# Post-norm transformer layer on eight cores: where the feed-forward weights' bf16 halves are cast from, and two waits of TensorE on VectorE

## The reference

```python
# x: (8, 2048, 1024) f32; one sequence per core
def reference(x, Wq, Wkv_down, Wk_up, Wv_up, Wo, W1, b1, W2, b2, scale):
    q = (x @ Wq.T).reshape(b, t, 8, 256)
    kv_latent = x @ Wkv_down.T                       # rank 64
    k, v = up-projections of kv_latent, 8 heads of 256
    attn = softmax(q k^T * 256 ** -0.5); out = attn v, concatenated @ Wo.T
    x = layernorm(x + out)
    # feed-forward, H = 4096, D = 1024
    lt = x[:, 1:17, :]; even, odd = lt[:, ::2], lt[:, 1::2]
    m1 = (even[:, :4, :, None] * odd[:, :4, None, :]).reshape(b, H, D)
    m2 = (even[:, 4:, :, None] * odd[:, 4:, None, :]).reshape(b, D, H)
    h = gelu(x @ W1.T + scale * einsum('bsd,bhd->bsh', x, m1) + b1)
    out = h @ W2.T + scale * einsum('bsh,boh->bso', h, m2) + b2
    return layernorm(x + out)
```

## Time and profile before

| what | us |
|---|---|
| three timed runs: median (lowest, highest) | 4390.7 (4057.57, 4457.24) |
| the profiled execution | 4037.43 |
| its span, first to last instruction, slowest core (core 0) | 4035.4 |
| spans of the eight cores | 4004.8 to 4035.4 |
| PE busy | 3134.8 (78%) |
| PEld busy | 1205.7 (30%) |
| DVE busy | 761.3 (19%) |
| ACT busy | 506.1 (13%) |
| POOL busy | 474.5 (12%) |

### The profile page before, as it was taken

How to read it: one execution, slowest core, us unless ns; L and a number is a source line. 1 busy time by engine, 2 the same in 40 slices (tenths; PEclk the granted TensorE clock), 3 DMA queues, 4 the chain that set the end, 5 groups by cost and what they waited for, 6 DMA issues and landing times.

```text
span 4035.4 us, 32628 instructions; the slowest of 8 cores (4004.8 to 4035.4 us)
## 1 busy us (share of the span) xinstructions
PE 3134.8 (78%) x10424; PEld 1205.7 (30%) x10610; DVE 761.3 (19%) x1123; ACT 506.1 (13%) x729; POOL 474.5 (12%) x728
## 2 busy tenths in 40 slices
PE   4657759979889889835667566569998899968997
PEld 1512223323323323301222222123443334423442
DVE  1111121121121121122222000023201331033201
ACT  0000004314324224200000000001000110011000
POOL 0000000000000000004564545500000000000000
PEclk8566679999999999967888777889998899989998
DMA  3130000010010010024775556533233332323232
GB/s 112 63 109 0 0 26 6 6 37 10 6 43 6 4 43 6 4 79 75 122 122 91 96 101 103 100 79 98 65 96 98 78 86 71 97 65 86 65 97 63
DMA packets 547944, 253.93 MB, mean 63 GB/s; under 512 B 264434, under 2 KB 526578, under 8 KB 546754
## 3 DMA queue, kind: packets, MB, share of 16 engines
q1 hardware_dynamic: 315938, 177.63, 16.7%
q0 software_dynamic: 79776, 32.20, 6.1%
q10 hardware_dynamic: 152064, 42.01, 4.7%
HBM read 211.05 MB, written 50.33 MB: 65 GB/s over the span
## 4 chain that ended last, share of the span: by engine, by line
PE 64%; DMA 11%; DVE 8%; issue 7%; POOL 6%; ACT 2%; SPq 1%; DVEq 0%; POOLq 0%; ACTq 0%
PE psU L592 11%; DMA whl<-w2p 6%; PE ps L337 4%; DMA whl<-w1p 4%; PE psY L624 3%; POOL whl L743 3%; PE ps L562 3%; PE ps L565 3%; POOL whl L793 3%; PE ps L558 3%; PE psY L976 2%; PE ps L1086 2%; PE ps L1091 2%; PE psY L1086 2%; PE psY L981 2%
## 5 line engine op out<-in xcount | busy, mean ns | idle before, releaser
L592 PE MATMUL psU<-et,kvtok 128*65 128x512 f32 x1024 | 523.1, 598 | 2.6
L578 ACT ACTIVATE et<-ps,Ubias 128x512 f32<-128x512 f32 x512 | 351.9, 687 | 643.3 <-PE psU L592 431.4
L1009 ACT ACTIVATE hgf<-htmp,b1s 128x512 f32<-128x512 f32 x128 | 92.4, 722 | 1680.7 <-DVE htmp L1003 1575.6
L1086 PE MATMUL ps<-hphi,whl 128*128 128x512 bf16 x500 | 203.4, 407 | 78.6 <-POOL whl L799 77.0
L1086 PE MATMUL psY<-hphi,whl 128*128 128x512 bf16 x504 | 205.0, 407 | 75.4 <-POOL whl L799 74.4
L976 PE MATMUL ps<-z1s,whl 128*128 128x512 bf16 x496 | 201.2, 406 | 61.8 <-POOL whl L749 61.1
L976 PE MATMUL psY<-z1s,whl 128*128 128x512 bf16 x505 | 209.9, 416 | 45.6 <-POOL whl L749 33.6
L981 PE MATMUL psY<-z1s,whl 128*128 128x512 bf16 x499 | 208.0, 417 | 9.9 <-POOL whl L749 5.4
L443 DVE RECIPROCAL rcp<-psU 1x512 f32<-1x512 f32 x32 | 107.4, 3355 | 573.1 <-PE psU L592 573.1
L1091 PE MATMUL psY<-hplo,whl 128*128 128x512 bf16 x500 | 203.8, 408 | 12.0 <-POOL whl L799 11.4
L1091 PE MATMUL ps<-hplo,whl 128*128 128x512 bf16 x504 | 205.0, 407 | 4.9 <-POOL whl L799 4.2
(11 more groups left out here) (172 smaller groups left out, 3115.0 us busy)
## 6 DMA issues: line engine op xcount, KB each, us to landing
whl<-w1sd SPq DMA_DIRECT2D x768, 64.0 KB, 2.2
whl<-w2sd SPq DMA_DIRECT2D x768, 64.0 KB, 2.0
w1f<-w1p SPq DMA_DIRECT2D x256, 64.0 KB, 3.5
w1sd<-whl ACTq DMA_DIRECT2D x512, 32.0 KB, 3.1
w2f<-w2p SPq DMA_DIRECT2D x256, 64.0 KB, 2.8
w2sd<-whl ACTq DMA_DIRECT2D x512, 32.0 KB, 2.6
xTs<-xT SPq DMA_DIRECT2D x8, 1024.0 KB
wst<-wq SPq DMA_DIRECT2D x16, 512.0 KB, 5.5
```

The lines of the kernel that those rows point to most:

```text
L578: P.op("scalar", lambda e, kc=kc, par=par, h=h: e.activation(out=et[:, par * 512:(par + 1) * 512], in_=psA[par][:], func=AF.Exp, bias=Ubia ...
L592: P.op("tensor", lambda e, kc=kc, par=par, h=h: e.matmul(psU[h % 2][:], kvtok[:, kc * 65:(kc + 1) * 65], et[:, par * 512:(par + 1) * 512], ...
L1086: P.op("tensor", lambda e, d=d, hi2=hi2, hc=hc, st=st: e.matmul(psP[d % 4][:], whl2[:, hi2: hi2 + 128], hphi[:, hc * 512:(hc + 1) * 512], ...
```

## The change

It does three things.

1. In the first block GpSimd no longer reads the weights from HBM a second time. One casting transfer per step reads the f32 tile that SP has loaded (`w1f`, `w2f`, in SBUF) and writes the high half. It takes the place of 8 transfers in a W1 step and of 4 in a W2 step. The wait for SP's load moves from the subtraction to this transfer.
2. The 8 matmuls at the start of a block (L923) waited for the newest DVE instruction, the last of the split of z1s, which they don't read. They now wait for the last read of their PSUM bank, the `u4t` of the block before.
3. The broadcast at every eighth step (L955) waited for the newest DVE instruction, the `hplo` of the step before. It now waits for the last read of its own bank, the `u_bc` copy of eight steps before.

```diff
+        cV_u4t_prev = [cV.n]
+        cV_ubc_g = [cV.n]
...
-            for c in range(DC):
-                P.op("gpsimd", lambda e, hc=hc, c=c, s4=s4: e.dma_start(
-                    out=whl1[:, s4 * 2048 + c * 128: s4 * 2048 + (c + 1) * 128],
-                    in_=w1p[hc, c * 128:(c + 1) * 128, :]),
-                    waits=[(cT, w1_free[s4]), (sST[s4], st1_done.get(s4, 0))],
-                    inc=sW1C[s % 2], inc_k=16)
+            P.op("gpsimd", lambda e, s=s, s4=s4: e.dma_start(
+                out=whl1[:, s4 * 2048: s4 * 2048 + 1024],
+                in_=w1f[:, s * DC * 128:(s + 1) * DC * 128]),
+                waits=[(sW1[s], dS_w1[(tb, hc)]), (cT, w1_free[s4]),
+                       (sST[s4], st1_done.get(s4, 0))],
+                inc=sW1C[s % 2], inc_k=16)
...
-                waits=[(sW1C[s % 2], dS_w1c[(tb, hc)]),
-                       (sW1[s], dS_w1[(tb, hc)]), (cT, w1_free[s4])], inc=cG)
+                waits=[(sW1C[s % 2], dS_w1c[(tb, hc)]), (cT, w1_free[s4])], inc=cG)
...
-            for k in range(4):
-                P.op("gpsimd", lambda e, d=d, g=g, k=k, s4=s4: e.dma_start(
-                    out=whl2[:, s4 * 1024 + k * 128: s4 * 1024 + (k + 1) * 128],
-                    in_=w2p[d, (g * 4 + k) * 128:(g * 4 + k + 1) * 128, :]),
-                    waits=[(cT, w2_free[s4]), (sSU[s4], st2_done.get(s4, 0))],
-                    inc=sW2C[s % 2], inc_k=16)
+            P.op("gpsimd", lambda e, s=s, s4=s4: e.dma_start(
+                out=whl2[:, s4 * 1024: s4 * 1024 + 512],
+                in_=w2f[:, s * 512:(s + 1) * 512]),
+                waits=[(sW2[s], dS_w2[(tb, d, g)]), (cT, w2_free[s4]),
+                       (sSU[s4], st2_done.get(s4, 0))],
+                inc=sW2C[s % 2], inc_k=16)
...
@@ the 8 matmuls into psL0 (L923) @@
-                    waits=[(cV, cV_E4), (cV, cV_norm2_prev2[0]), cV,
+                    waits=[(cV, cV_E4), (cV, cV_norm2_prev2[0]),
+                           (cV, cV_u4t_prev[0]),
                            (sZT[tb % 2], dS_z1tb[tb])],
...
             cV_u4 = cV.n
+            cV_u4t_prev[0] = cV_u4
...
@@ the broadcast into psL1 (L955) @@
-                        waits=[(sU4, dS_u4), (cV, cV_norm2_prev2[0]), cV], inc=cT)
+                        waits=[(sU4, dS_u4), (cV, cV_norm2_prev2[0]),
+                               (cV, cV_ubc_g[0])], inc=cT)
...
                     cV_ubc = cV.n
+                    cV_ubc_g[0] = cV_ubc
```

More of the change, by code:

```diff
@@ L802, in plan_w2 @@
                 whl2[:, s4 * 1024: s4 * 1024 + 512]),
-                waits=[(sW2C[s % 2], dS_w2c[(tb, d, g)]),
-                       (sW2[s], dS_w2[(tb, d, g)]), (cT, w2_free[s4])], inc=cG)
+                waits=[(sW2C[s % 2], dS_w2c[(tb, d, g)]), (cT, w2_free[s4])], inc=cG)
             cG_w2[tb * 64 + d * 8 + g] = cG.n
```

## The result

The changed kernel is faster: median 3805.09 us (3790.51 to 4016.62, 10 runs) against 4041.93 us (4026.54 to 4457.24, 10 runs) for the kernel before. The ratio is 0.9409 with a 95% interval of 0.9384 to 0.9433; I had forecast 3839 us and 0.951. In some executions of every kernel here one or both dies show a lower granted clock and take some per cent longer; comparisons leave those out, and in the profile of after it is die 1, so I read core 2 of both kernels. Core 2 is also free of a delay that core 0 of before had ahead of the feed-forward part.

A forecast was written before the change was run, and what follows sets the result against it. It took GpSimd's serial loop of issuing casts, awaiting landing and subtracting as the first block's bound, plus PE's waits for DVE. Gains 84 + 58 + 3 + 36.6 + 15.9 = 198 us; 4037.4 - 198 = 3839 us, range 3765 to 3945.

The forecast's parts named there:

- case A: First block: ScalarE binds W1, the shortened GpSimd loop binds W2; 3839 us, range 3800 to 3880, chance 0.60.
- F2: W2 stage: issue to landing of one casting transfer, 256 KB read; taken as 3.9 us, ends 2.8 and 4.8.
- a sign of being wrong: First block: new transfer landing over 6 us in W1, or under 3 or over 4.8 in W2.
- The allowance for traffic: W2 casting transfer: other traffic adds the median's excess over the minimum landing, 0.9 us.
- F1: W1 stage: issue to landing of one casting transfer, 512 KB read; 5.4 to 6.0 us.
- up to 13 us gained: End of W1 stage: PE runs ahead of ACT and begins the 96 small matmuls earlier; up to 13 us.
- The bubbles at steps 8, 16, 24: W1 stage: PE waits for DVE behind ACT's gelu, costing ACT's loop about 3 us each, 9 us lost.
- always released by issue: First block, sign in the profile after: ACT's gelu always released by issue.
- B: First block: short landing, ACT binds both stages; W2 gain 154 instead of 84 us, 3769 us, chance 0.17.
- C: First block: long landing, GpSimd binds both stages; steps 9.7 and 6.05 us, total 3922 us, chance 0.18.
- D: First block: SBUF casting transfer handled slowly row by row; slower, 4098 us at three times the by-element price, chance 0.03.
- E: Whole kernel: casts bring nothing, only the freed waits do; 3985 us, within 2%, chance 0.02.

The follow-up runs named there:

- short rows: Changed kernel with high and low halves interleaved, so the one casting transfer from SBUF has rows of 128 elements: 3858.8 us in its one run.
- the merged stores: Changed kernel with ScalarE's stores of a step in 2 transfers instead of 16 or 8: 3706.5, 3710.3 and 3731.5 us, ratio 0.9261.
- the casts alone: Changed kernel with parts 2 and 3 undone, leaving only the new casting transfers: 3875.7 us, ratio 0.9607.
- the waits alone: Kernel before with only parts 2 and 3 of the change, the two waits of TensorE: 3976.9 and 3977.8 us.
- eight from SBUF: Changed kernel with the cast from SBUF cut into 8 (W1) and 4 (W2) transfers, rows of 512 bytes: 3972.5 us.
- the HBM run: Changed kernel with the one casting transfer of a step reading f32 weights from HBM, rows of 512 bytes: 3858.8 and 3874.2 us, ratio 0.9599.
- the lookahead run: Changed kernel with GpSimd issuing the cast of step n+1 ahead of the subtraction of step n: 3800.5 us in one run.

## Why the prediction was right

The direction and case A held: ScalarE binds W1, the shortened serial loop binds W2, and the freed waits gave what their rows said. Measured 237 us off, forecast 198. That the total came so near is in part luck, for the two large terms missed in opposite ways: W2 gave 76 us more than forecast and W1 27 less.

- **W2, 84 us forecast, 160 measured on core 2.** The mechanism was right, its main term F2 was mis-sized: put at 3.9 us, measured 3.2 on average (median 2.9, just under the 3 that the prediction had named as a sign of being wrong). I priced the rows by elements, at today's 42 ns for 128 elements, so 168 ns for 512. The queue of the casting transfers gives the real price, by packets and share of 16 engines. First the landing after, core 2, then this queue in the W2 stage after (2143.2 to 2413.4 us), then with short rows (2173.0 to 2491.4 us):

```profile
DMA to landing us min/median/max: 2.3/2.9/4.7
...
q0 software_dynamic: 9072, 8.26, 18.7%
...
q0 software_dynamic: 33264, 8.26, 27.2%
```

  That is 0.187 x 270.2 x 16 / 9072 = 89 ns a packet after, and 0.272 x 318.4 x 16 / 33264 = 42 ns with short rows. A packet of 512 elements costs twice one of 128, not four times. Each engine works 9 packets of a transfer (8 rows and one more) in 0.80 us, where the short rows need 33 packets and 1.38 us; with the 0.2 us of the longer issue that is the whole difference of 0.8 in landing. The price by elements would have been that of the short rows, and their transfer does take 3.9 us on average (200.7/64 + 0.78). The allowance for traffic, 0.9 us, came to 0.6 (median less minimum). In all (5.15 - 4.29) x 63 = 54 us. The other 21 us are in the base: core 0 had steps of 6.49 us where core 2 had 6.82.
- **W1, 58 us forecast, 30.8 measured.** That ScalarE would bind was right, the merged stores show it. Its step was mis-sized, 8.85 us forecast and 9.51 measured from gelu to gelu. The 8.95 us between GpSimd's subtractions look like a hit and are none: from its first to its last subtraction GpSimd's lead over the gelus grew from 12.3 to 29.7 us, where before it went from 12.6 to 9.9. By the gelus the stage fell from 321.9 to 294.8 us, 27 us; the 20.0 us from the last gelu to the transfers became 16.6. Against the forecast 0.66 x 31 = 20 us are in the new step and 10 in the base (10.38 us on core 2, not 10.72); the end gave 3 back. The timeline of ScalarE's queue on core 2 shows what makes the step longer. It idles only 0.14 us a step, but the 16 issues take 7.93 us, against 7.10 in the three quickest steps: 49 of 496 take over 0.6 us. I had allowed 0.26 us a step for such. One of them, with its neighbours:

```profile
2004.36 0.46 ACTq L766 DMA_DIRECT2D w1sd<-whl  x1
2004.84 0.93 ACTq L762 DMA_DIRECT2D w1sd<-whl  x1
2005.80 0.48 ACTq L766 DMA_DIRECT2D w1sd<-whl  x1
```

  The slow issues come with the single transfer out of SBUF: 49 and 47 in the two runs of the change, 48 in the casts alone, 46 with short rows, 37 with the cast one step ahead, but 7 in the kernel before, 9 with the waits alone, 6 with one transfer from HBM and 11 with eight from SBUF (core 2 each). Why is open. In the HBM run, with the shorter W1 stage, the 16 issues take 7.29 us and ScalarE's step is 9.11.

  F1, put at 5.4 to 6.0, measured 104.6/32 + 0.57 = 3.8; it was off the path, so the error cost nothing. And of the "up to 13 us gained" at the end little came: from the last gelu to the last copy of the small products it was 18.7 us before and is 15.4 now. The last hplo and the copies after, core 2:

```profile
2122.91 0.69 DVE L1024 TENSOR_TENSOR hplo<-hgf,hphi 128x512 bf16<-128x512 f32 x1
2123.77 0.68 DVE L1051 COPY r<-ps 4x512 f32<-4x512 f32 x1 [0.17 <-DVE hplo L1024]
2124.62 0.68 DVE L1051 COPY r<-ps 4x512 f32<-4x512 f32 x1 [0.17 <-DVE r L1051]
2131.73 0.68 DVE L1051 COPY r<-ps 4x512 f32<-4x512 f32 x1 [6.43 <-PE ps L1046]
2136.91 0.68 DVE L1051 COPY r<-ps 4x512 f32<-4x512 f32 x1 [4.50 <-PE ps L1046]
```

  The first two products were ready early, but their copy stands in DVE's stream behind the last hplo, which waits for the last gelu, and the third product needs the bank that this copy frees. So PE's lead could be used for two of the four only. I had asked what PE waits for, not what its reader is queued behind.
- **The bubbles at steps 8, 16, 24** were forecast at about 3 us each. The gelus there are 12.0, 10.9 and 10.7 us apart, and ScalarE's queue idles 1.5, 1.0 and 1.6 us, so 4 us in all and not 9. The sign "always released by issue" was not met to the letter: the profile names issue 17 times, GpSimd 11 and DVE 3, but the queue hardly idles. The up to 24 us that PE waits there are mostly its own lead. Around step 8, core 2:

```profile
1885.73 0.72 ACT L1013 ACTIVATE hgf<-htmp,b1s 128x512 f32<-128x512 f32 x1 [8.93 <-issue]
1894.73 0.72 ACT L1013 ACTIVATE hgf<-htmp,b1s 128x512 f32<-128x512 f32 x1 [8.28 <-POOL whl L751]
1906.72 0.72 ACT L1013 ACTIVATE hgf<-htmp,b1s 128x512 f32<-128x512 f32 x1 [11.27 <-DVE htmp L1007]
```

- **Parts 2 and 3, 52.5 us forecast.** Right: 41.7 us in blocks 1 to 3 against 43, 12.7 at the first start against 11 to 12 (the casts' first issues included), and alone they gave 41.4 and 9.9 us there. Only the 4 us of the freed broadcast in the first block are not in the sum.
- **The rivals.** B (ScalarE binds both) needed F2 near 2.8; it came to 3.2 and ScalarE's 4.0 us a step was missed by 0.3 to 0.5. The lookahead run reaches exactly that bound. C, longer landings, is refuted by the landings themselves, though the W2 stage is in fact fuller, a DMA share of 0.72 after against 0.58 before (windows over the stage, core 2, after):

```profile
2143.00:2414.00 271.00, 190.36 (x770) 73.93 (x770) 5.25 (x7) 0.00 (x0) 106.42 (x127) 0.96 0.72 151
```

  D and E are out. By the fit of the Trainium skill, page "DMA: Bandwidth & Descriptors", section "Anatomy of one DMA — SWDGE (gpsimd) path", that the prediction cites, an estimate of F2 was 2.6 us and of F1 3.2; measured 2.9 to 3.2 and 3.7 to 3.8. For these long rows it was nearer than my 3.9 and 5.4. For the same bytes in short rows the runs measured 3.7 us from SBUF and 4.2 from HBM, which the fit, going by bytes alone, doesn't tell apart.

What stays open: why the W2 step with the old casts differs between cores and runs (6.42 to 6.82 us in the kernel before, 6.29 to 6.58 with the waits freed), why ScalarE's issues are slower beside the single transfer out of SBUF, and why the HBM source costs W2 0.4 to 0.5 us behind one transfer and nothing behind four.

## What to carry to other kernels

A loop of "issue, land, use" on one engine pays the landing in every step. Merge its transfers first, then give them long rows, then issue the next one ahead of the use; here these three and the source in SBUF took the W2 step from 6.3 to 4.0 us. Before counting the gain, price the issues of every engine that the faster loop will wait for: 16 store issues a step, off the path before, kept back three quarters of what the W1 stage could give (31 of 127 us came), and merging them brought another 96 us. Measure a stage by the engine that binds it: the starts of a producer that runs ahead through free slots (8.95 us apart here) show a shorter step than the stage has (9.51). A wait on "the newest instruction of that engine" is worth replacing by the last reader of the buffer, but only the part of the wait that nothing else in that engine's order repeats comes back.

## What was unexpected of the hardware

- The time for GpSimd to issue a casting transfer grows with its rows: 573 ns for 128 rows, 783 for 512, 917 for 1024 (line means; the last from the W1 stage with short rows). Four transfers of 128 rows cost 4 x 542.
- Rows of 512 bytes cost a casting transfer within SBUF 0.8 us of landing at 256 KB read, and 1.0 us at 512 KB (4.7 against 3.7), the longer issue included. A packet of 128 elements takes a DMA engine 42 ns on average, one of 512 elements 89, one of 1024 158 (0.159 x 277.4 x 16 / 4464, the W1 stage after, core 2): neither the price of a packet nor that of an element alone.
- Leaving out the second read of the weights from HBM (34 MB in all) did not shorten a W2 step while the number of transfers stayed the same (6.42 against 6.29 us); a W1 step it shortened by 0.4 us (9.85 against 10.22).
- ScalarE's issue of a store takes 0.45 us as a rule, but with the single cast out of SBUF running beside it one in ten took over 0.6 (49 of 496, against 6 of 496 with one cast from HBM).
